# The last unit but one of a fused attention and graph layer: z tile by tile, and a new order of the work on four engines

## What is computed

```python
x = layernorm(x + attention(x, adj))     # 12 heads of 32, scores masked where adj is 0
x = layernorm(x + digcn(x, adj))         # two layers l = 0, 1 of:
    u = h @ h.T / sqrt(384)                  # of one graph: 64 x 64
    delta = softmax(u) * adj
    attn = delta / (sum(delta) + 1e-10)
    ctx = (attn * upper) @ (h Wl + bl) + diag(attn) * (h Ws + bs) + (attn * lower) @ (h Wr + br)
    h = relu(layernorm(ctx, eps=1e-12) * g + b)
```

## Time and profile before

| | |
|---|---|
| median of 3 runs | 1282.78 us (1282.74 to 1283.77) |
| profiled execution, its time | 1282.98 us |
| its span in the trace | 1281.2 us |
| mean granted TensorE clock | 0.996 of full |
| TensorE busy | 1263.4 us, 99% of the span |
| `next_to_last` on TensorE | from 1206.02 to 1242.08 us |
| `last` on TensorE | from 1242.08 to 1271.78 us |

### The profile page before, as it was taken

The page is one execution under the profiler, slowest core; times in us unless marked ns, Lnnn a source line. Parts: engine busy times, 40 slices in busy tenths (PEclk is TensorE's granted clock), DMA queues, the critical chain, the costliest instruction groups (busy, mean ns, idle before and its releaser), DMA issues.

```text
span 1281.2 us, 34717 instructions
## 1 busy us (share of the span) xinstructions
PE 1263.4 (99%) x13844; PEld 1166.7 (91%) x13844; DVE 990.4 (77%) x2691; ACT 632.6 (49%) x1338; POOL 370.6 (29%) x401
## 2 busy tenths in 40 slices
PE   9999999999999999999999999999999999999986
PEld 8999999999999999999999999999999999999975
DVE  6777778777878777787778787777877777877877
ACT  6544554544554445545445545455454455454543
POOL 3322323232323222323223232223232232323211
PEclk9999999999999999999999999999999999999989
DMA  8211110111110111110111101111101111011000
GB/s 275 85 39 57 58 57 25 35 57 57 57 57 4 55 57 57 57 28 31 57 58 58 57 15 44 57 57 57 43 16 57 57 58 58 20 39 45 26 14 26
DMA packets 53072, 66.34 MB, mean 52 GB/s; under 512 B 17840, under 2 KB 39856, under 8 KB 52784
## 3 DMA queue, kind: packets, MB, share of 16 engines
q1 hardware_dynamic: 52768, 63.93, 16.5%
q10 hardware_dynamic: 144, 0.20, 0.0%
HBM read 38.54 MB, written 12.58 MB: 40 GB/s over the span
## 4 chain that ended last, share of the span: by engine, by line
PE 97%; DVE 1%; issue 1%; ACT 1%; POOL 0%; POOLq 0%; DVEq 0%; ACTq 0%
PE bank L420 25%; PE bank L422 23%; PE bank L421 23%; PE bank L623 7%; PE bank L569 4%; PE bank L532 4%; PE bank L517 3%; PE bank L498 3%; PE bank L545 2%; PE bank L555 2%; PE bank L603 1%; PE bank L631 0%; DVE probs L1222 0%; POOL probs L1727 0%; PE bank L745 0%
## 5 line engine op out<-in xcount | busy, mean ns | idle before, releaser
L420 PE MATMUL bank<-w_hi,hT_hi 128*128 128x384 f32 x1158 | 405.4, 350 | 0.2 <-ACT hT_hi L1048 0.2
L422 PE MATMUL bank<-w_hi,hT_lo 128*128 128x384 f32 x1158 | 390.3, 337 | 0.0
L421 PE MATMUL bank<-w_lo,hT_hi 128*128 128x384 f32 x1158 | 390.1, 337 | 0.0
L420 PEld LDWEIGHTS bank<-w_hi,hT_hi 128*128 128x128 f32 x1158 | 218.3, 189 | 6.6 <-issue 2.0
L421 PEld LDWEIGHTS bank<-w_lo,hT_hi 128*128 128x128 f32 x1158 | 218.9, 189 | 0.0
L422 PEld LDWEIGHTS bank<-w_hi,hT_lo 128*128 128x128 f32 x1158 | 218.3, 189 | 0.0
L1293 DVE TENSOR_TENSOR hlr<-bank,rows 128x384 f32<-128x384 f32 x256 | 142.3, 557 | 70.9 <-PE bank L422 68.0
L1740 POOL TENSOR_TENSOR ln_rstd<-ln_var,minus_half 128x2 f32<-128x2 f32 x125 | 96.2, 769 | 322.1 <-DVE ln_var L1386 113.8
L1727 POOL TENSOR_TENSOR probs<-probs,row_max 128x768 f32<-128x768 f32 x64 | 94.6, 1478 | 265.7 <-DVE row_max L1228 265.7
L1310 DVE TENSOR_TENSOR late<-bank,rows 128x384 f32<-128x384 f32 x128 | 71.3, 558 | 118.0 <-PE bank L422 117.9
L420 PE MATMUL bank<-xT_hi,w_hi 128*128 128x256 f32 x558 | 158.7, 284 | 0.0
(11 more groups left out here) (131 smaller groups left out, 2370.9 us busy)
## 6 DMA issues: line engine op xcount, KB each, us to landing
v_halves<-v_stage SPq DMA_DIRECT2D x128, 99.0 KB, 2.3
x_in<-in_x SPq DMA_DIRECT2D x32, 384.0 KB, 4.0
xT_in<-in_xT SPq DMA_DIRECT2D x31, 384.0 KB, 3.4
out<-late SPq DMA_DIRECT2D x31, 384.0 KB, 2.4
late<-in_w SPq DMA_DIRECT2D x7, 576.0 KB, 6.5
adj_in<-in_adj SPq DMA_DIRECT2D x32, 96.0 KB, 3.8
adjT_in<-in_adjT SPq DMA_DIRECT2D x64, 48.0 KB, 3.2
rows<-in_vectors SPq DMA_DIRECT2D x1, 1536.0 KB, 8.7
```

The costliest lines, as they stand in the source:

```text
L420: nc.tensor.matmul(o, l_hi, r_hi, start=first and n == 0, stop=False)
L421: nc.tensor.matmul(o, l_hi, r_lo, start=False, stop=False)
L422: done = nc.tensor.matmul(o, l_lo, r_hi, start=False, stop=final and n == last)
```

## The change

All of it concerns the step `next_to_last`, and helpers that `last` shares. (1) z of unit 30 goes tile by tile: statistics, inverse root, shift, normalization, transposition, relu, rounding and the gram matrix each for one tile, with helpers that until now only `last` used (`nth` counts their semaphores on over two units). Three matmuls and three ACTIVATEs of half the width replace one of the whole. The second tile's transposition goes into bank 2. (2) `mix(st, 0)` stands ahead of the self part of tile 1. (3) The heads (`attend`, `heads_out`) stand behind the first two sides of layer 1, and `transpose_h` at the step's end instead of within the sides. (4) ScalarE, VectorE and GpSimd get orders to match. The core of it:

```diff
 # TensorE
+            def next_transpose_z(st, t):
+                if t == 0:
+                    need(pe, self_ready, st.count(LATE, 4, 1))
+                else:
+                    need(pe, s_masked, st.count(MID, 4, 4))
+                need(pe, z_ready, st.count(LATE, 2, t + 1))
...
             def next_to_last(st):
 
                 gram(st, 0)
                 project_sides(st, 0)
                 transpose_e(st, 0)
                 project_self(st, 0, 0)
+                mix(st, 0)
                 project_self(st, 0, 1)
-                mix(st, 0)
                 transpose_probs(st)
+                next_transpose_z(st, 0)
+                next_gram(st, 0)
+
+                need(pe, self_ready, st.count(LATE, 4, 2))
+                project_side(st, 1, 0, LEFT)
+                next_transpose_z(st, 1)
+                project_side(st, 1, 0, RIGHT)
                 attend(st)
-                transpose_z(st)
-                gram(st, 1)
-                project_side(st, 1, 0, LEFT)
-                project_side(st, 1, 0, RIGHT)
+                next_gram(st, 1)
                 project_side(st, 1, 1, LEFT)
-                transpose_h(st)
                 project_side(st, 1, 1, RIGHT)
                 transpose_e(st, 1)
                 project_self(st, 1, 0)
                 project_self(st, 1, 1)
+                transpose_h(st)
                 mix(st, 1)
 # ScalarE
             def next_to_last(st):
                 exp_gram(st, 0)
                 exp_scores(st, 0)
+                scale_self(st, 0)
                 exp_scores(st, 1)
-                scale_self(st, 0)
                 scale_turned(st, 0)
+                last_z(st, 0)
+                next_take_z(st, 0)
+                last_z(st, 1)
                 take_pT(st)
-                normalize_inner(st)
-                take_zT(st)
-                split_zT(st)
+                next_take_z(st, 1)
                 exp_gram(st, 1)
                 normalize_h(st)
+                scale_self(st, 1)
                 take_hT(st)
                 split_hT_tile(st, 0)
-                scale_self(st, 1)
                 split_hT_tile(st, 1)
                 scale_turned(st, 1)
                 normalize_final(st)
 # VectorE
                 mask_aT(st, 0)
+                self_bias_tile(st, 0, 0)
+                need(dve, dz_ready, st.count(LATE, 2, 1))
+                make_ctx_first(st, LATE, 0)
+                last_z_stats(st, 0)
+                self_bias_tile(st, 0, 1)
+                last_shift(st, 0, ln1_mv, ln1_rstd, ln1_shift, z_rs, z_sh, nth(st, 0))
+                make_ctx_second(st, LATE, 0)
+                last_z_stats(st, 1)
+                last_shift(st, 1, ln1_mv, ln1_rstd, ln1_shift, z_rs, z_sh, nth(st, 1))
+                next_low(st, 0)
...
+                next_low(st, 1)
+                heads_out_tile(st, 0)
                 max_gram(st, 1)
+                heads_out_tile(st, 1)
                 sides_bias(st, 1, 0, LEFT)
                 sides_bias(st, 1, 0, RIGHT)
+                final_scale(st, 1)
+                stats_outer(st)
+                sides_bias(st, 1, 1, LEFT)
+                final_add(st, 0)
                 shift(st, MID, ln0_mv, ln0_rstd, ln0_shift, ln0_rs, ln0_sh)
-                final_add(st, 1)
-                take_diag(st, 1)
-                sides_bias(st, 1, 1, LEFT)
-                final_stats(st)
                 sides_bias(st, 1, 1, RIGHT)
                 mask_aT(st, 1)
+                take_diag(st, 1)
+                self_bias_tile(st, 1, 0)
+                final_add(st, 1)
+                self_bias_tile(st, 1, 1)
+                hT_low_tile(st, 0)
+                hT_low_tile(st, 1)
+                final_stats(st)
                 shift(st, FINAL, ln2_mv, ln2_rstd, ln2_shift, ln2_rs, ln2_sh)
-                self_bias_tile(st, 1, 0)
-                hT_low_tile(st, 0)
-                self_bias_tile(st, 1, 1)
-                hT_low_tile(st, 1)
```

More of the change, by code:

```diff
@@ L648, in second, with next_gram @@
                 scores(st, EARLY)
+            def next_transpose_z(st, t):
[4 more added lines that the diff above has]
+                need(pe, z_ready, st.count(LATE, 2, t + 1))
+                for kc in range(KC):
+                    done = nc.tensor.transpose(NEXT_Z_BANKS[t][:, kc * P:(kc + 1) * P],
+                                               c0[:, t, kc * P:(kc + 1) * P], ident[:, :])
+                done.then_inc(hT_psum, 1)
+            def next_gram(st, t):
+                need(pe, hT_ready, st.count(LATE, 5, 3 if t == 0 else 5))
+                for kc in range(KC):
+                    for g in range(GRAPHS):
+                        a = hT[:, t, kc, g * N:(g + 1) * N]
+                        done = nc.tensor.matmul(U_BANK[1][g * N:(g + 1) * N, t * N:(t + 1) * N], a, a,
+                                                start=kc == 0, stop=kc == KC - 1)
+                if t == T - 1:
+                    done.then_inc(u_psum, 1)
             def next_to_last(st):
@@ L1012, in second, with next_take_z @@
                 split_hT(st)
+            def next_take_z(st, t):
+                need(act, hT_psum, st.count(LATE, 4, 3 + t))
+                need(act, u_psum, st.count(LATE, 2, 1))
+                need(act, hTlo_ready, st.count(LATE, 4, 2))
+                need(act, self_psum, st.count(LATE, 4, t + 1))
+                for kc in range(KC):
+                    done = nc.scalar.activation(hT[:, t, kc, :], NEXT_Z_BANKS[t][:, kc * P:(kc + 1) * P], ACT.Relu,
+                                                bias=b0_col[:, kc:kc + 1], scale=g0_col[:, kc:kc + 1])
+                    if kc == KC - 1:
+                        done.then_inc(hT_ready, 1 + t)
+                need(act, hT_ready, st.count(LATE, 5, 3 if t == 0 else 5))
+                nc.scalar.activation(hT_hi[:, t], hT[:, t], ACT.Copy).then_inc(hThi_ready, 1)
             def next_to_last(st):
@@ L1593, in last @@
                 last_sum_stats(end, 1)
-                last_shift(end, 1, ln2_mv, ln2_rstd, ln2_shift, y_rs, y_sh)
+                last_shift(end, 1, ln2_mv, ln2_rstd, ln2_shift, y_rs, y_sh, 1 + 1)
             def step(st):
```

70 lines of the change are left out of this document (36 added, 34 removed).

## The result

The changed kernel is slower: 1287.84 us as the median of 7 runs (1286.75 to 1288.01) against 1282.74 of the kernel before (7 runs, 1281.92 to 1283.91). The ratio is 1.0036 with a 95% interval of 1.0025 to 1.0047, so 5.1 us. The direction was forecast. The size was not: the median lies 2.2 us above the forecast (1285.6) and 0.4 above the top of its range, nearest to the rival "both stops lower the clock" (1287.1). In microseconds the interval is 3.2 to 6.0: the forecast of +2.8 lies outside it, the top of the range (+4.6) inside.

What follows compares the result with a forecast made beforehand. TensorE, busy 1263.4 of 1281.2 us, was taken to bound the kernel through its idling and its clock. Terms -4.2 - 2.9 + 3.9 + 0.5 + 3.2 + 2.6 gave +3.1, followed as times +2.8: 1285.6 us, range 1282.5 to 1287.4.

Steps and rivals of the forecast that it cites:

- both stops lower the clock: Rival: the clock falls at z's waits and at the turned matrix; +4.3 us, 1287.1 us; chance 0.28.
- the turned matrix: In `last`, TensorE stands still 3.2 us because `final_stats` and its `shift` are queued ahead of `make_ctx` on VectorE.
- The new waits: TensorE idle 1.6 us before z's first tile, 1.6 before the gram half, 0.7 before the first side; together 3.9 us.
- the first side of `last`: At the start of `last`, the first side waits 0.5 us for VectorE's `hT_low`.
- the order: Sum without clock: old waits -4.2, waits in z +3.9, first side of `last` +0.5, turned matrix +3.2 us.
- The old clock fall: Before the change, TensorE works 5.9 us at half speed from 1226.3 to 1232.2; removing it gives -2.9 us.
- the clock never falls: Rival: transpositions count as activity, so the clock stays up; +0.2 us, 1283.0 us; chance 0.20.
- The first fall: Around z's new waits the clock falls, 2.8 to 6.4 us at half speed; +2.6 us, lower bound 0.
- The second fall: A clock fall at the turned matrix's stop, costing about 1.5 us, bounds 0 and 2.9; left out of the likeliest sum.
- the likeliest case: Old waits and old fall gone, new waits and a first fall only; +2.8 us, 1285.6 us; chance 0.42.
- transpositions count: Premise for the first stop: if transpositions are activity, idle pieces are only 1.6, 1.6 and 0.7 us, with no fall.
- GpSimd's root: Root behind `stats_outer`, with a `final_add` beside it, might take 1.00 instead of 0.69 us; 0.3 us kept for the range.

Runs made afterwards that it cites:

- stats_first: Changed kernel with `final_stats` of the last step but one ahead of the two `hT_low_tile` on VectorE; 1284.52 us, ratio 1.0013.
- fill_both: Changed kernel with unread matmuls in both stops, 14 in the first and 16 in the second; 1283.65 us, ratio 1.0005.
- fill_before: Kernel before the change with 12 and 7 unread matmuls in its stops of 2.3 and 1.4 us; 1281.25 us, ratio 0.9987.
- fill_first: Changed kernel with 14 unread matmuls in the first stop, 8 ahead of z's first tile, 6 ahead of the first gram half; 1285.66 us, ratio 1.0024.
- after_again: The changed kernel itself, unaltered, measured again beside other runs; 1286.65 us, ratio 1.0028.
- fill_transposed: Changed kernel with 19 unread transpositions of 128 columns in the first stop (10 ahead of z, 9 ahead of the first gram half); 1285.24 us, ratio 1.0016.
- copies_first: Changed kernel with `take_hT` and the two roundings of h ahead of `scale_self` of tile 1 on ScalarE; 1285.40 us, ratio 1.0023.
- z_ahead: Changed kernel with `last_z` of tile 0 ahead of `scale_turned` of inner layer 1 on ScalarE; 1287.10 us.

## Why the prediction missed

**The path was worked out rightly.** The signs named beforehand all came: no wait over 1.7 us up to 1224 (the longest is 1.51), the longest wait of the run at the turned matrix for `hlr`, VectorE idle for GpSimd (0.80 us) ahead of `make_ctx`, and the clock down within 1222 to 1230. The new waits were put at 1.6, 1.6 and 0.7 and measured 1.51, 1.25 and 0.33 (0.67 where the clock was up); the first side of `last` at 0.5, measured 0.35; the turned matrix at 3.2, measured 3.14, through the very chain that was named (stats_first takes 2.0 us of it away). As a whole the order was put at -4.2 + 3.9 + 0.5 + 3.2 = +3.4 us; with the clock up the new order takes 64.79 us and the old one 62.07 (fill_both, fill_before), so +2.7.

**The old clock fall** was put at -2.9; filling the old stops gave 2.18. The term took half of 5.9 us, where work at the low level loses 0.46 of its time, and it left out that a wait of 0.47 us for `hT_lo` lay hidden behind the slow gram matrix. This error of 0.7 and that of the order are opposite and cancel, in part because the 0.47 us stand in both: "the clock never falls" was +0.5 by the prediction's pieces (+0.2 followed as times), and fill_both's sum is 0.54 above before's.

**The first fall** was put at +2.6. Piece b of the changed kernel against fill_first's is 2.53, a's 0.05: 2.58. Right, though partly by luck, since another execution shows 1.6 in b (after_again, 16.38 against 14.79).

**The second fall is the step that failed.** Its price was right (1.5; measured 1.56), but the likeliest case had it at nothing, with the words "clean idling between dense matmuls" and "a little shorter than 3.7 us". The 3.7 us were counted from the end of the heads to the old fall, with 0.85 us of transpositions taken as idleness. fill_transposed shows that transpositions, in the first stop at least, kept the clock up as matmuls did. The longest time without any work was 2.3 us in the kernel before, and the new stop of 3.1 us is longer than that, not shorter. So the ground for leaving the second fall out was not there, and the rival at 1287.1 deserved more than its 0.28. In every profile here with a stop of 2.68 us or more in front of the turned matrix (after, after_again, copies_first, fill_first, fill_transposed, z_ahead) the clock was down in d; in the eight others, with a stop of 1.11 us or less or none, it was not.

The other half of the prediction's argument fails too: it took "transpositions count" to mean "no fall in the first stop". They kept the clock up where they filled the stop, and yet in every profile that left the first stop open it fell, around idle pieces of 1.51 and 1.25 us with 0.5 us of transpositions between them (0.37 and 1.85 us in z_ahead). So the longest single piece of idleness doesn't decide it either. What does was not found out.

The sum with measured terms: 64.25 (before) - 2.18 (old fall) + 2.72 (order) + 2.58 (first fall) + 1.56 (second fall) = 68.93, and the profile has 68.92. The first two terms give fill_both's sum by their making; what the agreement shows is that the two falls, each priced with only its own stop filled, add to it.

**GpSimd's root.** The 0.3 us kept for it did not come: the root behind `stats_outer` took 0.71 us, the one in the stop 0.69. The first of these had a `final_add` (two operands in SBUF) beside it for 0.4 us, as the prediction feared, and neither took longer than it does alone (0.69 and 0.55 us in other rows):

```profile
1237.25 0.71 POOL L1803 TENSOR_TENSOR ln_rstd<-ln_var,minus_half 128x2 f32<-128x2 f32 x1 [1.84 <-DVE ln_var L1296]
1237.55 0.55 DVE L1429 SCALAR_TENSOR_TENSOR late<-late,h 128x384 f32<-128x384 f32 x1
```

In stats_first, with VectorE at `hT_low` (two operands in SBUF) at the same time, it took 0.93:

```profile
1242.77 0.93 POOL L1803 TENSOR_TENSOR ln_rstd<-ln_var,minus_half 128x2 f32<-128x2 f32 x1 [4.83 <-DVE ln_var L1436]
```

In this case `hT_low` (from 1242.59) had begun ahead of the root; in the other the root had begun first. It cost nothing in stats_first, since the root lay beside work that VectorE had to do anyway. Its cause was not tested by itself. The pair of ports that VectorE and GpSimd share, one of them at a time, is described by the Trainium skill ("SBUF — State Buffer", section "SBUF: two separate sides"); the 0.93 us fit it, while the `final_add` that took its usual 0.55 beside the root doesn't show the wait that the rule would give it.

**What stays open.** Behind one and the same stop the low stretch begins at another moment and is longer in some executions (b of after and after_again, d of after and fill_first). Behind the stop of 3.14 us the clock fell 4.0 us after the stop had begun and stayed down for 3.4 us in after, but 2.4 us after and for 6.8 us in fill_first. Why was not settled, and so the medians of kernels with falls follow their profiles only to about a microsecond.

## What to carry to other kernels

Where TensorE is busy for 98% of the time, price a stop with its clock: here a stop of 3.1 us lost 4.7. Count as idle only what is idle; matmuls that nobody reads kept the clock in both stops here, and transpositions did in the first, the only one where they were tried. And look at what stands in a queue between a late input and the instruction that the next stage waits for: moving one call by two places was worth 2 to 3 us (4.0 to 5.1 over before became 2.0), while the one local repair of an early wait that was tried alone (z ahead of `scale_turned`) only moved the wait to the next semaphores.

## What the runs showed of the hardware

19 transpositions of 128 columns in two idle pieces of 1.5 and 1.25 us kept TensorE at 2.4 GHz as 14 matmuls of 384 columns did (fill_transposed and fill_first, 14.78 and 14.79 us in b); with the pieces left idle b took 16.34 to 17.32. A stop of 2.68 us (copies_first) was followed by 1.2 GHz, beginning at about 1248.0, 0.6 us after work had begun again, so that dense work paid for it:

```profile
1247.50:1248.00 0.50, 0.50 (x4) 0.50 (x5) 0.43 (x4) 0.00 (x0) 0.11 (x1) 0.95 0.00 0
```

At 1.2 GHz the matmuls of 384 columns began 0.32 us apart and at 2.4 GHz 0.174, a factor of 1.84 and not 2, so a low stretch of 3.4 us in dense work cost 1.56 us and not 1.7.

Unread matmuls in the stops made the unchanged old order 1.4 us faster (fill_before), although they add work to the engine that bounds the kernel.
